# Four-block kernel on one core: in the third block, values computed turned and last of the side work, output statistics by pairs of row tiles, keys repeated on the other partitions by DMA

## What is computed

```python
    h = norm_scale * x / (nrm + EPS) * split_scale
    q = (h @ Wq.T).reshape(b, s, H, dh)          # H = 8 heads, dh = 64
    k = (h @ Wk.T).reshape(b, s, G, dh)          # G = 2 groups
    v = (h @ Wv.T).reshape(b, s, G, dh)
    ...
    scores = jnp.einsum('bghsd,bgtd->bghst', q, k) / np.float32(np.sqrt(dh))
    attn = jax.nn.softmax(scores, axis=-1)
    out = jnp.einsum('bghst,bgtd->bghsd', attn, v)
    out = out.reshape(b, H, s, dh).transpose(0, 2, 1, 3).reshape(b, s, H * dh)
    return x + out @ Wo.T
```

## Time and profile before

| | us |
|---|---|
| median of 3 runs | 1569.31 (1569.26 to 1570.19) |
| the profiled execution, its own time | 1568.97 |
| its span in the trace | 1567.0 |
| PE busy | 1453.4 (93% of the span) |
| DVE busy | 1014.7 (65%) |
| ACT busy | 819.9 (52%) |
| POOL busy | 730.3 (47%) |

### The profile page before, as it was taken

The page is one execution under the profiler, slowest core; times in us unless marked ns, Lnnn a source line. Parts: engine busy times, 40 slices in busy tenths (PEclk is TensorE's granted clock), DMA queues, the critical chain, the costliest instruction groups (busy, mean ns, idle before and its releaser), DMA issues.

```text
span 1567.0 us, 21347 instructions
## 1 busy us (share of the span) xinstructions
PE 1453.4 (93%) x7252; PEld 1187.5 (76%) x7252; DVE 1014.7 (65%) x2044; ACT 819.9 (52%) x1574; POOL 730.3 (47%) x970
## 2 busy tenths in 40 slices
PE   5999999989999999999999996699899999999996
PEld 4888788767787878787878774577788888888874
DVE  5888789677879797988888775445332424424233
ACT  4666557578777777878787763321222213212221
POOL 4788546545454545555454444123324333243332
PEclk9999999999999999999999999799999999999998
DMA  7465023320002020202020201322011010110100
GB/s 207 130 160 135 21 95 107 108 81 1 1 10 73 1 81 2 81 1 81 1 81 1 101 1 54 111 84 67 2 54 53 1 54 0 54 54 0 54 28 27
DMA packets 46205, 88.51 MB, mean 56 GB/s; under 512 B 2720, under 2 KB 3744, under 8 KB 46112
## 3 DMA queue, kind: packets, MB, share of 16 engines
q1 hardware_dynamic: 42416, 79.98, 14.9%
q0 software_dynamic: 3696, 7.34, 2.9%
HBM read 62.14 MB, written 25.17 MB: 56 GB/s over the span
## 4 chain that ended last, share of the span: by engine, by line
PE 73%; DVE 13%; POOL 5%; issue 4%; ACT 3%; DMA 2%; SPq 0%; POOLq 0%; DVEq 0%; ACTq 0%
PE f_inner L57 23%; PE context L1629 12%; PE f_down L2055 9%; PE context L57 7%; PE score L57 5%; PE turned L1664 5%; PE score L851 4%; PE context L1692 2%; PE context L1690 2%; DVE g_ptl L1551 2%; DVE g_neg_max L1537 2%; PE turned L57 1%; DVE f_wl L1979 1%; POOL g_prob L1247 1%; PE f_inner L2027 1%
## 5 line engine op out<-in xcount | busy, mean ns | idle before, releaser
L1247 POOL TENSOR_SCALAR g_prob<-g_prob,g_inv_sum 128x512 f32<-128x512 f32 x256 | 177.7, 694 | 298.4 <-DVE g_inv_sum L1542 298.3
L57 PE MATMUL f_inner<-f_xth,f_wh 128*128 128x512 f32 x704 | 281.3, 400 | 15.4 <-DVE f_wl L1979 12.7
L57 PE MATMUL f_inner<-f_xtl,f_wh 128*128 128x512 f32 x704 | 280.0, 398 | 0.0
L1889 ACT ACTIVATE f_silu<-f_inner,f_inner_scale 128x512 f32<-128x512 f32 x88 | 60.7, 689 | 414.0 <-PE f_inner L57 414.0
L1948 DVE SCALAR_TENSOR_TENSOR f_hidden<-f_inner,f_inner_scale,f_silu 128x512 f32<-128x512 f32 x88 | 66.0, 750 | 313.8 <-PE f_inner L57 313.8
L1837 POOL TENSOR_TENSOR f_hl<-f_hidden,f_hh 128x512 fp32r<-128x512 f32 x88 | 127.9, 1453 | 297.0 <-DVE f_hh L1954 297.0
L1537 DVE TENSOR_REDUCE g_neg_max<-score 128x1 f32<-128x512 f32 x256 | 175.4, 685 | 84.0 <-PE score L57 82.8
L1368 ACT ACTIVATE g_prob<-score,g_neg_max 128x512 f32<-128x512 f32 x256 | 176.6, 690 | 95.7 <-DVE g_neg_max L1537 93.4
L1551 DVE TENSOR_TENSOR g_ptl<-turned,g_pth 128x512 fp32r<-128x512 f32 x256 | 173.9, 679 | 17.2 <-ACT g_pth L1416 15.1
L1664 PE MATMUL turned<-identity,g_prob 128*128 128x128 f32 x1024 | 156.9, 276 | 26.9 <-DVE g_ptl L1551 26.9
L57 PEld LDWEIGHTS f_inner<-f_xth,f_wh 128*128 128x128 f32 x704 | 133.3, 189 | 54.2 <-DVE f_wl L1979 17.3
(11 more groups left out here) (230 smaller groups left out, 3393.6 us busy)
## 6 DMA issues: line engine op xcount, KB each, us to landing
xt<-x_t SPq DMA_DIRECT2D x16, 512.0 KB, 6.2
x_mixed<-x_resident SPq DMA_DIRECT2D x8, 1024.0 KB, 4.3
x_pair<-x_mixed SPq DMA_DIRECT2D x8, 1024.0 KB, 8.0
g_res<-x_mixed SPq DMA_DIRECT2D x8, 1024.0 KB, 6.7
x_attended<-g_res SPq DMA_DIRECT2D x8, 1024.0 KB, 5.2
x_pair<-x_attended SPq DMA_DIRECT2D x8, 1024.0 KB, 5.6
x_resident<-x SPq DMA_DIRECT2D x7, 1024.0 KB, 10.9
factor_sum<-factors POOLq DMA_DIRECT2D x7, 1024.0 KB, 10.8
```

Source lines behind the costliest of these rows:

```text
L57: last = nc.tensor.matmul(out, lhsT, rhs, start=(n == 0), stop=(n == len(pairs) - 1))
L1247: nc.gpsimd.tensor_scalar(prob[:, at, :], prob[:, at, :], inv_sum[:, at:at + 1], 1.0, ALU.mult, ALU.mult).then_inc(prob_ready, 1)
```

## The change

- `v` is now made turned, under the name `vt`: Wv is held and the turned input streamed, 12 matmuls with 512 columns. ACT copies the result to `v_turned`, PE turns it back with four transposes (`turn_v`, the new `v`, at the head of the next batch's side work), and ACT and DVE split that as before. `vt` stands last in the list.
- The list is in another order (`k` ahead of `wo3`), with other rooms in each unit.
- The output statistics, scales, norms and additions go by pairs of tiles. `NORM` was units 24 to 27 and is now 19, 20, 28 and 29; `ADD` was 25 to 28 and is now 20, 21, 29 and 30.
- ACT copies only the half of the keys that lies in place, and SP sends four transfers (64 partitions of 2 KB each) to the other half.

```diff
-NAMES = ["q1", "q2", "q3", "h0", "h1", "wo0", "wo1", "h2", "h3", "wo2", "wo3", "k", "v", "q0"]
+NAMES = ["v", "q1", "q2", "q3", "h0", "h1", "wo0", "wo1", "h2", "h3", "wo2", "k", "wo3", "q0", "vt"]
 SPLIT = [name for name in NAMES if name[0] != "w"]
+OWN = ("v", "q1", "q2", "q3")
...
-H = (5, 6, 10, 11)
-CONVERT = (20, 24, 32, 39)
-SHARE, SHARE_BESIDE_OUT = 8, 4
+H = (5, 6, 8, 11)
+CONVERT = (25, 26, 32, 39)
+SHARE, SHARE_AT_END, SHARE_BESIDE_OUT = 8, 7, 3
...
-    waiting = [(name, {"h": 1, "v": 3 * T * T}.get(name[0], 3 * T)) for name in NAMES]
-    at = 0
+    waiting = [(name, 1 if name[0] == "h" or name == "v" else 3 * T) for name in NAMES]
+    at = room = 0
     for u in range(UNITS):
         shares.append([])
-        room = SHARE_BESIDE_OUT if (u - OUT_LAG) % T < 2 else SHARE
-        while waiting and room > 0:
+        room = min(room, 0) + (SHARE_BESIDE_OUT if (u - OUT_LAG) % T < 2 else SHARE if u < 6 * T else SHARE_AT_END)
+        while waiting and room >= 0.5:
             name, count = waiting[0]
-            cost = {"h": 2, "v": 0.5}.get(name[0], 1)
+            cost = 2 if name[0] == "h" or name == "v" else 1
             i = NAMES.index(name)
-            earliest = [end[n] + (2 if n[0] == "w" else 3) for n in NAMES[i - 2:i - 1] if n in end]
+            earliest = [end[n] + (2 if n[0] == "w" else 3) for n in NAMES[max(i - 2, 0):max(i - 1, 0)] if n in end]
             earliest += {"wo0": [CONVERT[-1] - UNITS + 2], "k": [end.get("h3", 0) + 3],
-                         "h0": [H[0] + 2], "h1": [H[1] + 2]}.get(name, [])
+                         "h0": [H[0] + 2], "h1": [H[1] + 2], "h2": [H[2] + 2], "h3": [H[3] + 2]}.get(name, [])
             if at == 0 and earliest and max(earliest) > u:
                 break
-            step = min(count - at, max(1, int(room / cost)))
+            step = min(count - at, max(1, int(room / cost + 0.5)))
...
-AHEAD = sum(name[0] in "hkv" or name == "q0" for name in NAMES)
+AHEAD = len(SPLIT) - len(OWN)
 WO = [END[f"wo{t}"] for t in range(T)]
 RESIDUAL = [at - 1 for at in WO]
-NORM = [WO[-1] + 4 + t for t in range(T)]
+NORM = [WO[1] + 4, WO[1] + 5, WO[3] + 4, WO[3] + 5]
 ADD = [at + 1 for at in NORM]
 
 
-def side_at(name):
-
-    return (AHEAD + SPLIT.index(name)) % 2 if name in SPLIT else (AHEAD + NAMES.index(name) + T) % 2
+LAG = {"vt": 1}
...
                 if first:
+                    repeat_k(-1, 1)
                     rest.store_last()
                 if not first:
                     sp.wait_ge(stored, b * 16)
...
                     if last:
                         sp.wait_ge(h_ready, B * T)
                         fetch(sp)
+                if not last:
+                    repeat_k(b, p)
+                if not first:
                     store(b - 1)
+
+            def repeat_k(b, p):
+                sp.wait_ge(side_free, side_use(b, "k") + 1)
+                for part in (kh, kl):
+                    for g in range(GROUPS):
+                        sp.dma_start(part[HALF[1 - g], 1 - p, g, :].bitcast(F32),
+                                     part[HALF[g], 1 - p, g, :].bitcast(F32)).then_inc(k_repeated, 16)
...
-            def output_scales(b):
-                wait_alone(pool, s, ostats, b + 1)
-                row_scales(nc, s, pool, omv, ove[:, :], ors[:, :], oshift[:, :], s.minus_half[:, :],
-                           opool, b * 2).then_inc(oscales, 1)
+            def output_scales(b, i):
+                half = slice(2 * i, 2 * i + 2)
+                pool.wait_ge(ostats, 2 * b + i + 1)
+                row_scales(nc, s, pool, omv[:, half, :], ove[:, half], ors[:, half], oshift[:, half],
+                           s.minus_half[:, half], opool, b * 4 + i * 2).then_inc(oscales, 1)
...
-                if u == WO[-1] + 2 and not first:
-                    output_scales(b - 1)
-                if u in ADD and not first:
+                for i in range(2):
+                    if u == WO[2 * i + 1] + 2 and not first:
+                        output_scales(b - 1, i)
+                if u in ADD and not first and not drain:
...
                     for g in range(GROUPS):
-                        for half in HALF:
-                            last = nc.scalar.copy(kh[half, 1 - p, g, :], src[HALF[g], :])
+                        last = nc.scalar.copy(kh[HALF[g], 1 - p, g, :], src[HALF[g], :])
+                elif name == "vt":
+                    last = nc.scalar.copy(v_turned[:, :], src[:, :])
                 else:
-                    last = nc.scalar.copy(v[:, 1 - p, :, :, 0:DH],
+                    last = nc.scalar.copy(v[:, p, :, :, 0:DH],
...
-                if t == 0:
-                    act.wait_ge(oscales, b + 1)
+                if t % 2 == 0:
+                    act.wait_ge(oscales, 2 * b + t // 2 + 1)
...
+                if name == "vt":
+                    dve.wait_ge(side_free, side_use(b, name))
+                    dve.sem_inc(side_free, 1)
+                    return
...
-                if t == T - 1:
-                    wait_alone(dve, s, side_free, use + 1)
-                    for t in range(T):
+                if t % 2 == 1:
+                    dve.wait_ge(side_free, use + 1)
+                    for t in (t - 1, t):
...
+            def turn_v(b, use):
+                side_bank(use)
+                pe.wait_ge(side_hi, side_split(b - 1, "vt"))
+                for t in range(T):
+                    cols = slice(t * P, (t + 1) * P)
+                    last = nc.tensor.transpose(side[use % 2][:, cols], v_turned[:, cols], s.identity[:, :])
...
-                    k, n, bank_cols = m // 3 % T, m % 3, slice(0, N)
-                    if name == "v":
-                        cols = bank_cols = slice(m // (3 * T) * P, (m // (3 * T) + 1) * P)
-                        pairs = split(hth[:, k, cols], htl[:, k, cols], wvh[:, k, :], wvl[:, k, :])
-                    elif name == "k":
-                        pairs = split(wkh[:, k, :], wkl[:, k, :], hth[:, k, :], htl[:, k, :])
+                    k, n = m // 3, m % 3
+                    if name in ("k", "vt"):
+                        wh, wl = (wkh, wkl) if name == "k" else (wvh, wvl)
+                        pairs = split(wh[:, k, :], wl[:, k, :], hth[:, k, :], htl[:, k, :])
...
-            side_share(-1, "v", 0, 3 * T * T, True)
             pe.wait_ge(own.wq_lo, T)
             side_share(-1, "q0", 0, 3 * T, True)
+            side_share(-1, "vt", 0, 3 * T, True)
...
-                        pe.wait_ge(side_free, side_use(b, "q1"))
-                        pe.wait_ge(k_repeated, b + 1)
+                        pe.wait_ge(side_free, side_use(b - 1, "q0") + 1)
+                        pe.wait_ge(k_repeated, (b + 1) * 64)
```

More of the change, by code:

```diff
@@ L1031, in side_use @@
     if isinstance(b, int) and b >= B - 1 and name[0] == "w":
-        missing = [n for n in NAMES[:j] if n[0] != "w" and (b == B or n[0] != "q")]
+        missing = [n for n in NAMES[:j] if n in SPLIT and (b == B or n not in OWN)]
         j -= len(missing) + (AHEAD if b == B else 0)
@@ L1047, in side_done @@
 def side_done(u, first, last, drain, lag):
-    return [name for name in NAMES if END[name] + lag == u and side_runs(name, first, last, drain)]
+    return [name for name in NAMES if END[name] + min(lag, LAG.get(name, lag)) == u
+            and side_runs(name, first, last, drain)]
 def side_runs(name, first, last, drain):
@@ L1055, in side_runs @@
         return not first
-    return not drain and (not last or name in ("q1", "q2", "q3"))
+    return not drain and (not last or name in OWN)
 def attention_fetch(nc, s, stack, norm_scale, split_scale, wq_t, wk_t, wv_t, wo_t, x_in):
@@ L1135, in grouped_attention @@
         kh, kl, v, pth, ptl, oh, ol = own.kh, own.kl, own.v, own.pth, own.ptl, own.oh, own.ol
-        v_lo_part, xn = own.v_lo_part, own.xn
+        v_lo_part, xn, v_turned = own.v_lo_part, own.xn, own.v_turned
         x, prob, total, out_sum, feature = s.x_pair, s.prob, s.total, s.out_sum, s.feature
@@ L1338, in hi_of @@
                 act.wait_ge(side_ready, side_use(b, name) + 1)
-                src = side[side_at(name)]
+                src = side[side_at(b, name)]
                 if name[0] == "h":
@@ L1429, in step @@
                     v_lo_of(b * HEADS + done // T, done // T)
-                if u == END["k"] + 4 and not last and not drain:
-                    repeat_k_lo(b, p)
                 if u in NORM and not first:
@@ L1603, in side_share @@
             def side_share(b, name, start, end, done):
-                use, out = side_use(b, name), side[side_at(name)]
+                use, out = side_use(b, name), side[side_at(b, name)]
                 if name[0] == "h":
                     return turn_h(b + 1, use, int(name[1]))
+                if name == "v":
+                    return turn_v(b, use)
                 if start == 0:
@@ L1628, in side_share @@
                                  split(oh[:, k, cols], ol[:, k, cols], woh[:, k, :], wol[:, k, :]))
```

(2 more changed lines are left out.)

25 lines of the change are left out of this document (12 added, 13 removed).

## The result

The changed kernel takes 1571.34 us (median of 20 runs, 1568.82 to 1574.89), the kernel before 1569.64 in the same comparison (20 runs, 1567.13 to 1571.54). The ratio is 1.0014, with a 95% interval of 1.0008 to 1.0021: slower, by 1.7 us between the medians. I had said 1568.3. The execution that was profiled is the slowest of the 20 (1574.89, a span of 1573.1), so I took a second profile of the same kernel (1570.07 us, span 1568.3); what follows is of the first, unless the second is named.

What follows compares the result with a forecast made beforehand. PE's own work was taken as the bound, with some waits for DVE. Terms -2.1 - 3.0 - 2.6 + 5 x 2.5 - 4.5 - 1.8 + 0.5 gave -1.0 us: 1568.3 us, range 1556 to 1577.

Steps and rivals of the forecast that it cites:

- So a batch with nothing else late takes 80.1 - 2.0 - 0.5 = 77.5, or -2.6: Third block's batch: v saves PE 2.0 us, waits go from 4.5 to 4.0, making 77.5 us.
- to the first score: Before the first batch: vt takes 2.76 us where v took 5.2, less 0.3 for the key transfers: -2.1 us.
- batch 0: Third block's first batch: v's 2.0 us less and lighter clusters, -3.0 us (bounds -2.0 and -4.0).
- last batch and end together: Last batch: more even work, -4.5 us (bounds 0 and -6); end: two norms leave the tail, shorter power, -1.8 us.
- Base of a batch: PE's work in a batch of the kernel before, 75.6 us plus 4.5 waiting; the change takes off 2.0 and 0.5.
- The keys at nothing: In each batch: ACT's dropped key copies priced at nothing, covered by its 18 us of idle time.
- The keys before the first batch: Key transfers land at 315 to 317, PE wants them at 316.1: 0.3 us, bounds 0 and 1.5.
- The late load: Start of batches 2 to 6: x's load behind the later store, statistics at +9.2 us, costing 5.1 us a batch.
- The clock: PE's idle stretch in batches 2 to 6 drops its clock: 0.1 us each, bounds 0 and 1.2, +0.5 in all.
- A: Rival, batches 2 to 6: x's load is hidden anyway; 1543 us with the wait gone, 1554 with 2.8 off each; chance 0.17.
- B: Rival, units 3 to 8 of batches 2 to 6: lower clock outlasts DVE's backlog, 1.5 to 2.5 us each, 1578; chance 0.15.
- C: Rival: load doesn't limit, DVE's 67.6 us match badly, a batch gains 1 us in place of 2.6; 1579; chance 0.10.

Runs made afterwards that it cites:

- load_first: The changed kernel with SP's load of the next x issued ahead of the store of the attended batch: 1547.91 us, ratio 0.9859.
- after_fill_tail: The changed kernel with 34 matmuls that nothing reads in PE's waits at the end of the third block: 1570.91 us, ratio 1.0002.
- lf_vt_pieces: load_first with each of vt's 12 matmuls a batch cut into four of 128 columns: 1566.02 us, ratio 0.9973.
- add_early: The changed kernel with norms and additions of the second pair of tiles one unit earlier: 1569.13 us, ratio 0.9995.
- fill_wait: The changed kernel with 11 unread matmuls in PE's wait at the end of unit 2 of batches 2 to 6: 1575.7 us, ratio 1.0045.

## Why the prediction was wrong, step by step

I forecast 1.0 us less on the span; the median became 1.7 longer. The mechanism that I said decides was right in place, length and number of times. What failed is the step **"So a batch with nothing else late takes 80.1 - 2.0 - 0.5 = 77.5, or -2.6"**: such a batch takes 78.0, or -2.1, and it comes six times; I counted 0.5 too much in each: 3.0 us. All terms, against the second profile (a span 1.3 us over that of before):

| term | forecast | second profile |
|---|---|---|
| to the first score | -2.1 | -1.07 |
| batch 0 | -3.0 | -3.88 |
| batch 1 | -2.6 | -2.07 |
| batches 2 to 6, clock in them | +12.5 + 0.5 | +14.72 |
| last batch and end together | -6.3 | -6.55 |
| fourth block | 0 | +0.15 |
| sum | -1.0 | +1.30 |

The sum is 2.3 us off. The base accounts for 3.0, the way to the first score for 1.0; the first batch gave 0.9 more than I had, and the load with its clock cost 0.8 less. The line of the last batch and the end agrees in part by luck: the last batch gave 3.8 where I had 4.5, the end 2.75 where I had 1.8. In the first profile the last batch gave 5.1 and the end took 2.4 more than before.

- **Base of a batch, wrong in size.** As the profile counts it, PE is busy 75.14 us in load_first's batch; in the one of the earlier trace rows 76.9, so it lost 1.8, not 2.0. Its waits went from 3.3 to 2.9 us (the 80.2 and 78.0 less what it is busy), not from 4.5 to 4.0. Together that is some 2.2. My 75.6 and 4.5 were counted from starts, so only the differences compare.

The waits of one batch, in load_first, grouped by who ended them (us, times, longest):

```profile
PE turned L1691 <- DVE g_ptl L1570: 1.2, 3, 0.6
PE context L1616 <- DVE g_obn L1511: 0.9, 1, 0.9
PE context L1624 <- DVEq L1482: 0.7, 1, 0.7
```

I had 0.5 in unit 0 (measured 0.7), 2.4 in units 8 to 10 (1.2), and 1.1 in unit 17 (0.9).

- **The keys at nothing, wrong.** They are worth 0.77 us a batch, 6.4 to 7.0 in all. In my 77.5 this was hidden, since I followed a batch whose ACT was already free of them. So what I took for v and the waits is in part the keys': without them a batch has 78.78 us, or only 1.4 less than before. The idle total of an engine, which was my reason, was no cover in the units where its work stands close.
- **The keys before the first batch, about right.** PE waits 0.57 us for them; I had 0.3, bounds 0 and 1.5. From the issue of the load of x to the first score it is 10.95 us (306.19 to 317.14) in place of 12.78 (305.86 to 318.64): 1.8 less, where I had 2.1. The rest of what the table shows there lies in the blocks before, and is scatter: in six profiles of the changed kernel and its variants, alike up to there, the first score starts between 316.8 and 318.5 us.

```profile
317.14 0.47 PE L57 MATMUL score<-g_kh,g_q 128*128 128x512 f32 x1 [0.57 <-DMA g_kl<-g_kl]
```

- **The late load, right.** Statistics at 9.2 was my forecast, 8.7 to 10.9 is measured, 9.6 in the mean; 5.1 us a batch, and 5.3 and 5.0 in the two profiles (83.27 and 83.07 less 78.0). PE's waits were to be 3.4 and 1.0; the batch shown has 3.1 and 0.7. The further 0.7 in unit 5 shows only where the clock stays up.
- **The clock, right in size.** I argued that a stretch at the lower level falls into time in which PE would wait, and gave it 0.1 us. The runs show 0 to 0.1 where the batch's mean clock was 0.98 and 0.4 to 0.6 where it was 0.96, some 0.2 in the mean. I had it fall five times; it fell in five batches of the first profile and in four of the second. That the clock matters at the block's end I had left out.
- **Rivals.** A, the hidden load, didn't come, but load_first is what it describes: 1547.9, where I worked out 1543; the same 0.5 in each of six batches is 3 of the 5 us. B's 1.5 to 2.5 us each time didn't come: it is 0.6 at most in the two profiles, and came near once in after_fill_tail (1.3). C's mechanism, that DVE bounds the batch, fell with load_first and lf_vt_pieces, but its direction was right: the rest did give less than I counted, 2.1 us a batch, between my 2.6 and C's 1.

Two things together made a change that saves 21.7 us (load_first against before) into one that loses 2: the last addition comes two units later, and in SP's queue the load of x stands behind the store that waits for it. Neither is seen in the diff's lines on v.

## What to carry to other kernels

When a change moves the last step of a chain that ends in a store, look at what stands behind the store in the same queue, and move that before you judge the change: here it decided between 1571 and 1548 us. A load with no slack shows in the profile of before as an engine that takes its data within a tenth of a microsecond of the landing, and in this kernel nearly every microsecond of delay from there on was paid. And price a helper engine's work where it stands: 17 us of idle time in a batch didn't cover 2.2 us of copies in a stretch where three jobs met. When you move a step forward, look whether its inputs are there: in add_early ACT waited 1.3 us for scales that the changed kernel found ready.

## What was unexpected in the hardware

- **The same kernel differs by 5 us in one stretch.** The end of the block took 29.1 us in one profile of the changed kernel and 23.9 in the other, with mean clocks of 0.86 and 0.78 in the one and 1.00 in the other.

- **A kernel can be slower in a block that no edit touches.** fill_wait's 5.4 us over the second profile of the changed kernel lie, all but 0.7, at the start of the fourth block. The fourth block to its third batch's first transposes, and the rest, in the second profile and in fill_wait:

```profile
983.56:1170.50 186.94, 166.78 (x684) 131.58 (x685) 79.73 (x105) 46.21 (x57) 52.35 (x38) 0.94 0.19 65
1170.50:1568.26 397.76, 383.37 (x1689) 308.39 (x1687) 145.36 (x284) 91.73 (x139) 138.67 (x139) 0.99 0.09 32
```

```profile
984.29:1175.96 191.67, 169.83 (x684) 133.70 (x685) 79.75 (x105) 46.20 (x57) 52.27 (x38) 0.92 0.19 64
1175.96:1573.70 397.74, 383.35 (x1689) 308.44 (x1687) 145.36 (x284) 91.65 (x139) 138.26 (x139) 0.99 0.09 32
```

The same 684 matmuls, 4.7 us apart. At one place PE waits for nothing that the profile shows, once in the second profile, twice in fill_wait:

```profile
1110.83 0.49 PE L57 MATMUL f_inner<-f_xth,f_wh 128*128 128x512 f32 x1 [2.86 <-issue]
```

```profile
1111.63 0.49 PE L57 MATMUL f_inner<-f_xth,f_wh 128*128 128x512 f32 x1 [2.89 <-issue]
...
1114.55 0.79 PE L57 MATMUL f_inner<-f_xth,f_wh 128*128 128x512 f32 x1 [1.72 <-issue]
```

From 1113.7, within the second wait, to 1120.4 the granted clock is 0.50. In lf_vt_pieces the one wait takes 5.0 us (2.6 to 3.8 in the other twelve profiles), and its fourth block 588.0 (584.4 to 585.7 in those). This is no luck of one execution: all five runs of fill_wait (from 1575.5 up) are slower than each of the changed kernel's 21 (up to 1574.9). What the wait is for stays open. Transfers of instructions (16 KB each) stand around it, and both kernels have more PE instructions ahead of it than the changed one; but so have the filled kernels and the one before, so that this is the reason isn't shown.

- **Filling a wait with useless matmuls helps only where PE itself is late.** At the end of the block it gave 1.6 to 2.5 us in medians, in batches 2 to 6 little (415.9 us against 416.3 and 415.3), and nothing at the fourth block's start.
- **Transfers within the on-chip memory are quick.** 128 KB from 64 partitions to the other 64 landed 2.3 us after their issue (median of 16, the longest 4.3), though each pair holds SP's queue for 1.2 us.

```profile
g_kh<-g_kh SPq DMA_DIRECT2D x16, 128.0 KB, 2.3
```
